# A two-layer graph-attention kernel: step placing and input sums moved from VectorE and ScalarE to GpSimd, the first normalisation halved, keys and values begun before the degrees are known

## The chip, the cores and the metric

One NeuronCore of a Trainium2 chip runs the whole program; the other cores are idle. The metric is the device time of one execution in microseconds (us), and below, times without a unit are microseconds from the start of the profiled execution's span. Engines: TensorE (PE; its weight loads are shown apart as PEld), VectorE (DVE), ScalarE (ACT), GpSimd (POOL) and SyncE (SP, which here only issues transfers). SBUF is the on-chip memory, a PSUM bank holds 128 x 512 float32 of TensorE's results.

## What is computed

3125 nodes with 128 features, 103125 directed edges sorted by target, two layers. The parts that matter here:

```python
h = relu(layernorm(x))                      # the layers' input
for l in range(2):
    xn  = layernorm(x, ln1_g[l], ln1_b[l])
    deg = segment_sum(ones, src); deg = (deg - deg.mean()) / (std(deg) + 1e-6)
    xp  = xn + xn @ Wpos[l] + bpos[l] + deg[:, None] * Wdeg[l][0] + bdeg[l]
    q, k, v = xp @ Wq[l] + bq[l], xp @ Wk[l] + bk[l], xp @ Wv[l] + bv[l]
    att   = clip(nan_to_num((q[dst] * k[src]).sum_per_head / 4), -50, 50)
    alpha = softmax over the edges of one dst
    x = x + segment_sum(v[src] * alpha, dst) @ Wo[l] + bo[l]
    x = x + gelu(layernorm(x, ln2_g[l], ln2_b[l]) @ W1[l] + b1[l]) @ W2[l] + b2[l]
return x_in + x
```

## The kernel before, in words

The nodes are 25 blocks of 128. The edges are tiles of 128, four tiles to a group, 202 groups a layer; for each tile GpSimd issues one indirect DMA (L765) that fetches 128 rows of keys and values (256 floats) from a table in DRAM (`kv_table`) into a ring of eight groups (`kvr`). That makes 1612 gathers for both layers. Group n may be fetched only when the message of group n-8 is done (`s_msg`, L1552). For each group, ScalarE makes one-hot matrices from `relT` (`edge_spread`, L1172 and L1176), TensorE spreads the queries (`edge_q`, L1005), VectorE multiplies and reduces (L1534, L1538, L1552), TensorE sums (L1018), and VectorE adds to `agg` (L1561). Dense work of finished blocks lies between. `relT` has two buffers; each load (`rel_rows`, L610) serves two of the first groups, so groups 0 to 3 use the first two loads and groups 4 and 5 the third.

Before the first gather there is a preparation of some 110 us, whose order is written out by hand:

- VectorE makes a histogram of the edge sources in 16 steps, each two instructions of one-hot digits in bf16 (L1217, 3328 and 2600 elements), which TensorE sums (L792, 26 matmuls a step, `s_hist_oh` and `s_hist_mm`, two buffers). Other work stands between the steps by step number k: the ranking of the blocks (`rank_blocks`), the statistics of the input, the placing of steps (`place_steps`, L1266 to L1294), the scaling of the query weights (`scale_queries`), the folding of the position weights (`fold_positions`, L1314), the first layer's variance (`first_layer_var`, L1239 to L1242).
- ScalarE passes over the input five times, 25 instructions each: sums (L1053), squares about the mean (L1056), normalise and rectify with sums (L1061), squares of that (L1070), the first layer's normalisation (L1076). Then it takes the transposed blocks out of PSUM (L1083), the transposed tile numbers (`rel`, `srcidx`, L1088) and the bias of keys and values (L1091).
- GpSimd waits for `tileno`, the last product that it needs of `place_steps` (L1290), fetches 7 + 7 tiles of targets and sources (L726), splits the biases in three bf16 parts (L730 to L735), and turns the fetched integers to floats and subtracts the block's base (L738, L739, L743, L745). TensorE transposes these (`turn_rows`, L835). A memset of `agg` (L749) follows.
- When the histogram is done, TensorE and ScalarE make the degrees and their spread. Then VectorE writes keys and values for 13 pairs of blocks: for each block degree times weight plus bias (L1368), for each pair the sum with TensorE's product in PSUM (L1381, product L853). SyncE stores each pair to the table (L621). GpSimd's first gather waits for all 13 stores.
- Then come the queries (TensorE L862 with the bias in L780, VectorE L1602 into two buffers `q_nat`), and SyncE moves each block to its rank's place (L627, 25 transfers). The first `edge_q` waits for these.

SyncE issues in program order, and it waits in that order too: behind the row for ranks come 25 transfers of the normalised input to its ranked place (`x`, L591), then biases, `rel_table`, `relT` twice, the 13 stores, the 25 query moves, and then the third `relT`.

## Time and profile before

| | |
|---|---|
| time, median of three (lowest to highest) | 2205.68 us (2205.52 to 2209.19) |
| time of the profiled execution | 2207.93 us |
| span of the profiled execution | 2206.2 us |
| busy in the span: DVE, POOL, PE, ACT | 1716.4, 1578.3, 1417.7, 933.9 us |
| mean granted TensorE clock | 0.807 of full speed |

Times of instructions are those of the profiled execution. A group line gives out<-in by the program's names, the count, busy time and mean, and the idle time of the engine just before these instructions with what ended it. Two instructions on one engine overlap a little, so starts are a better measure of pace than durations.

### The profile page before, as it was taken

How to read it: one execution, taken by the hardware profiler on the slowest of the kernel's cores; microseconds unless marked ns; L12 is line 12 of the kernel's file. 1: busy time of each engine (PE TensorE's matmuls, PEld its weight loads, DVE VectorE, ACT ScalarE, POOL GpSimd, SP SyncE). 2: the span in 40 equal slices, each digit the busy share in tenths (PEclk: the TensorE clock that was granted, in tenths of full speed). 3: DMA queues.
4: the chain of work that ended last, by engine and by line, in shares of the span. 5: the costliest groups of instructions: out<-in, count | busy, mean ns of one | idle time of the engine just before them, and what ended most of it. 6: DMA issues, size and time to landing. Idle time of an engine off the chain costs nothing.

```text
span 2206.2 us, 32470 instructions
## 1 busy us (share of the span) xinstructions
PE 1417.7 (64%) x8220; PEld 1243.9 (56%) x8220; DVE 1716.4 (78%) x5109; ACT 933.9 (42%) x2172; POOL 1578.3 (72%) x1669
## 2 busy tenths in 40 slices
PE   5766566665766666666666656666665766566666
PEld 4555565555655555565555556555555655555564
DVE  7849888887788878887866777777777778777776
ACT  7424353543435353534543334334353435344343
POOL 6277777777777777777726777777777777777773
PEclk9769888888878878877877777778798779778778
DMA  3355444444444444454424444444444444444442
GB/s 101 99 162 164 141 134 148 129 144 134 134 145 128 148 134 143 128 148 134 136 62 125 134 134 134 129 134 138 134 128 134 137 134 128 134 134 138 125 138 57
DMA packets 123505, 289.30 MB, mean 131 GB/s; under 512 B 31524, under 2 KB 57056, under 8 KB 123328
## 3 DMA queue, kind: packets, MB, share of 16 engines
q0 software_dynamic: 77824, 212.31, 33.3%
q1 hardware_dynamic: 45504, 74.92, 10.4%
q8 instruction: 76, 1.25, 0.2%
q14 instruction: 101, 0.83, 0.1%
HBM read 275.44 MB, written 8.38 MB: 129 GB/s over the span
## 4 chain that ended last, share of the span: by engine, by line
POOL 57%; issue 21%; DVE 7%; PE 7%; DMA 4%; ACT 3%; DVEq 0%; POOLq 0%; SPq 0%; ACTq 0%
POOL kvr L765 57%; DMA kvr<-kv_table,srcidx 3%; PE bank L1005 2%; PE bank L1018 2%; DVE agg L1561 2%; DVE kvr L1217 1%; DVE prod L1534 1%; DVE msg L1552 1%; ACT apart L1172 1%; ACT x_nat L1061 1%; ACT onehotT L1176 0%; ACT agg L1076 0%; PE bank L930 0%; DVE kvr L1368 0%; PE bank L949 0%
## 5 line engine op out<-in xcount | busy, mean ns | idle before, releaser
L765 POOL DMA_INDIRECT kvr<-kv_table,srcidx x1612 | 1531.6, 950 | 558.8 <-issue 481.7
L1005 PE MATMUL bank<-q,onehotT 128*128 x3328 | 611.1, 341 | 726.1 <-DVE prod L1534 478.8
L1005 PEld LDWEIGHTS bank<-q,onehotT 128*128 128x128 f32 x3328 | 520.3, 238 | 829.1 <-issue 828.7
L1018 PE MATMUL bank<-msg,onehot 128*128 128x136 f32 x3328 | 609.9, 343 | 3.4 <-DVE msg L1552 3.3
L1181 ACT ACTIVATE bank<-attc 128x32 f32<-128x32 f32 x404 | 81.2, 201 | 1194.0 <-DVE attc L1547 1193.4
L1018 PEld LDWEIGHTS bank<-msg,onehot 128*128 128x128 f32 x3328 | 571.0, 251 | 5.9 <-DVE msg L1552 5.7
L1534 DVE TENSOR_TENSOR prod<-kvr,bank 128x512 f32<-128x512 f32 x404 | 276.9, 685 | 306.6 <-DMA kvr<-kv_table,srcidx 272.6
L1561 DVE TENSOR_TENSOR agg<-agg,bank 128x136 f32 x1628 | 471.6, 290 | 44.7 <-PE bank L1018 38.2
L1172 ACT ACTIVATE apart<-relT,minus_p 128x512 bf16<-128x512 bf16 x416 | 293.8, 706 | 0.5
L1527 DVE TENSOR_TENSOR onehot<-bank,rel 128x512 f32<-128x512 f32 x416 | 283.1, 683 | 0.4
L1552 DVE TENSOR_TENSOR msg<-kvr,bank 128x512 f32<-128x512 f32 x404 | 274.8, 680 | 2.8 <-ACT bank L1181 2.6
L1538 DVE TENSOR_REDUCE att<-prod 128x32 f32<-128x512 f32 x404 | 274.0, 678 | 0.1
L1176 ACT ACTIVATE onehotT<-apart 128x512 f32<-128x512 bf16 x416 | 261.9, 629 | 13.1
L1184 ACT ACTIVATE msg<-attc 128x32 f32<-128x32 f32 x404 | 86.0, 213 | 0.0
L1543 DVE TENSOR_SCALAR attc<-att 128x32 f32<-128x32 f32 x404 | 78.2, 194 | 0.0
L1547 DVE COPY_PREDICATED attc<-attnan,zeros 128x32 f32<-128x32 uint8 x404 | 77.2, 191 | 0.0
L1542 DVE TENSOR_TENSOR attnan<-att 128x32 uint8<-128x32 f32 x404 | 74.6, 185 | 0.1
L1427 DVE TENSOR_TENSOR x<-x,bank 128x384 f32<-128x384 f32 (+1 forms) x36 | 18.9, 525 | 67.6 <-PE bank L780 67.5
L1181 ACT ACT_TABLE_LOAD x52 | 66.7, 1283 | 0.9
L961 PE MATMUL bank<-w,hT 128*128 128x128 f32 x400 | 57.1, 287 | 3.4 <-issue 2.8
L949 PE MATMUL bank<-xnT,w 128*128 128x384 f32 (+1 forms) x144 | 57.6, 531 | 1.6 <-ACT xnT L1112 1.3
L1217 DVE TENSOR_TENSOR kvr<-kvr,q 128x3328 bf16<-128x3328 bf16 (+1 forms) x32 | 53.1, 1715 | 1.7 <-ACT q L1047 1.3
(205 smaller groups left out, 854.6 us busy)
## 6 DMA issues: line engine op xcount, KB each, us to landing
relT<-rel_table SPq DMA_DIRECT2D x104, 512.0 KB, 4.2
kvr<-kv_table,srcidx POOLq DMA_INDIRECT x1612
qkv<-kv_table SPq DMA_DIRECT2D x25, 128.0 KB, 3.4
kv_table<-qkv SPq DMA_DIRECT2D x25, 128.0 KB, 3.0
kv_table<-kvr SPq DMA_DIRECT2D x12, 256.0 KB, 2.1
w<-weights SPq DMA_DIRECT2D x2, 840.0 KB, 7.6
loops<-x_in SPq DMA_DIRECT2D x5, 320.0 KB, 5.6
x<-x_nat SPq DMA_DIRECT2D x25, 64.0 KB
```

The lines of the kernel that those rows point to most:

```text
L765: pool.indirect_dma_start(kvr[:, n % RING, j, :], None, kv_table[l], bass.IndirectOffsetOnAxis(ap=srcidx[:, step:step + 1], axis=0)).then_ ...
L1005: mm = pe.matmul(bank[2][:, j * D:(j + 1) * D], onehotT[:, m % OHT, j, :], q[:, bass.ds(ranks[j + h], 1), :].rearrange("p a c -> p (a c)") ...
L1018: mm = pe.matmul(sum_ps(n, k), onehot[:, m % OH, j, :], msg[:, n % 2, j, :], start=(m, j) == of[0], stop=(m, j) == of[-1])
L1172: act.activation(apart[:], relT[:, m // BODY % 2, r, :], ACT.Abs, bias=minus_p[:]).then_inc(s_apart, 1)
L1176: act.activation(onehotT[:, m % OHT, :, :].rearrange("p j e -> p (j e)"), apart[:], ACT.Relu, bias=1.0, scale=-1.0).then_inc(s_ohT, 1)
L1181: act.activation(ex, attc[:, n % 2, :], ACT.Exp).then_inc(s_ex, 1)
L1184: act.activation(msg[:, n % 2, :, D:AGG], attc[:, n % 2, :].rearrange("p (j h) -> p j h", h=H), ACT.Exp).then_inc(s_den, 1)
L1527: dve.tensor_tensor(onehot[:, m % OH, :, :], iota_ps.unsqueeze(1).broadcast_to([P, G, P]), rel[:, row:row + G].unsqueeze(2).broadcast_to([ ...
L1534: dve.tensor_tensor(prod[:], kvr[:, n % RING, :, 0:D], bank[2][:].rearrange("p (j c) -> p j c", c=D), ALU.mult).then_inc(s_prod, 1)
L1538: dve.tensor_reduce(att[:, n % 2, :], prod[:].rearrange("p j (h d) -> p (j h) d", d=HD), AX, ALU.add).then_inc(s_att, 1)
L1552: dve.tensor_tensor(by_head(msg[:, n % 2, :, 0:D]), by_head(kvr[:, n % RING, :, D:KV]), ex.rearrange("p (j h) -> p j h", h=H).unsqueeze(3) ...
L1561: dve.tensor_tensor(target, target, sum_ps(n, j), ALU.add).then_inc(s_agg, 1)
```

## The change

- `input_sums` (new, GpSimd): the sum over the 128 features of each of 25 blocks as seven tensor additions of 1600, 800, 400, 200, 100, 50 and 25 elements a partition. The ScalarE pass of sums is gone; the pass of squares is about the row's first element instead of its mean, so that it needs no mean, and VectorE corrects for it (`input_var`, four instructions for three).
- `scale_queries` (ten small instructions) and the greater part of `place_steps` (eleven) go to GpSimd. VectorE keeps `begin_blocks` at k = 2 and `number_steps` at k = 4, which waits for GpSimd (`s_within`). `tileno` comes out of `number_steps`. GpSimd fetches the targets, splits the biases, then fetches the sources.
- The first layer's statistics are made in two halves, blocks 0 to 11 (k = 4) and 12 to 24 (k = 8), the reciprocals in the middle of the steps 2, 5 and 9.
- TensorE transposes blocks 0 to 11 at k = 6 and 7, the rest at k = 11 and 12, the tile numbers at k = 13 and 14, all four in bank 5 one after the other. Keys and values of pairs 0 to 3 are made before or beside the degrees, and VectorE keeps them with their bias (`keep_early`); the degree is added for each block when it is known (`add_degrees`, one instruction a block for all 25). Pairs 4 to 12 get the bias from a matmul. The extra pass of L1381 is gone.
- SyncE: the 25 `x` transfers stand behind the query moves, and so ahead of the third `relT`. The second layer's folding comes behind the queries on TensorE and VectorE.

The diff cut to its core:

```diff
+            def input_sums():
+                for k in range(X_LOADS):
+                    pool.wait_ge(s_x[k], 16)
+                half = D // 2
+                pool.tensor_tensor(x_nat[:, :, 0:half], x_raw[:, :, 0:half], x_raw[:, :, half:D], ALU.add).then_inc(s_sums_in, 1)
+                for k in range(1, SUM_STEPS):
+                    half //= 2
+                    pool.wait_ge(s_sums_in, k)
+                    target = x_sums[:, 0, :].unsqueeze(2) if half == 1 else x_nat[:, :, 0:half]
+                    pool.tensor_tensor(target, x_nat[:, :, 0:half], x_nat[:, :, half:2 * half], ALU.add).then_inc(s_sums_in, 1)
...
+            input_sums()
+            scale_queries()
+            place_steps()
+            pool.wait_ge(s_tileno, 1)
+            fetch_rows(step_dst, dst_tiles)
+            split_bias()
+            fetch_rows(step_src, src_tiles)
...
-                act.activation(x_nat[:, b, :], x_raw[:, b, :], ACT.Identity, accum_out=x_sums[:, 0, b:b + 1]).then_inc(s_sums_in, 1)
-            act.wait_ge(s_mean_in, 1)
-            for b in range(BLOCKS):
-                act.activation(x_nat[:, b, :], x_raw[:, b, :], ACT.Square, bias=shift[:, b:b + 1], accum_out=x_sums[:, 1, b:b + 1]).then_inc(s_sums_in, 1)
+                act.activation(xn_nat[:, b, :], x_raw[:, b, :], ACT.Square, bias=x_raw[:, b, 0:1], scale=-1.0, accum_out=x_sums[:, 1, b:b + 1]).then_inc(s_squares_in, 1)
...
+            rectify(*HALVES[0])
+            square(*HALVES[0])
...
+            rectify(HALVES[1][0], middle)
+            first_layer_root(0)
+            rectify(middle, BLOCKS)
+            first_layer_norm(0)
+            square(*HALVES[1])
+            for c in range(3):
+                untranspose_nat(c)
+            first_layer_root(1)
...
             for k in range(HSTEPS):
-                hist_step(k)
+                hist_low(k)
+                if k == 2:
+                    scale_and_shift(0, 0, BLOCKS)
+                elif k == 5:
+                    scale_and_shift(1, *HALVES[0])
+                elif k == 9:
+                    scale_and_shift(2, *HALVES[1])
+                hist_high(k)
...
+                    begin_blocks()
+                elif k == 4:
+                    number_steps()
+                    first_layer_var(0)
...
+            def add_degrees(i):
...
+                    of = to[:, j, :] if i < KV_EARLY else bank[k][:, j * KV:(j + 1) * KV]
+                    ins = dve.scalar_tensor_tensor(out=to[:, j, :], in0=u_deg[:, 0, D:3 * D], scalar=deg[:, 0, b0 + j:b0 + j + 1], in1=of, op0=ALU.mult, op1=ALU.add)
...
-            sp.wait_ge(s_relu, BLOCKS)
-            for b0, nb in NAT:
-                for j, r in enumerate(read_block_ranks(ENG.SP, b0, nb)):
-                    sp.dma_start(x[:, bass.ds(r, 1), :], x_nat[:, b0 + j:b0 + j + 1, :]).then_inc(s_x_ranked, 16)
```

Where instructions stand. On GpSimd, between its constants and the first gather, before:

```order
L716 COPY hT<-ident 64x64 x2
L721 COPY hT<-w 128x128 x2
L726 DMA q<-dst_tiles,tileno 128x128 x7
L726 DMA q<-src_tiles,tileno 128x128 x7
L730 CAST bias_bf<-bias_col 128x10
```

and now, in the same place:

```order
L749 TENSOR_TENSOR x_nat<-loops 128x25x64
L754 TENSOR_TENSOR x_nat<-x_nat 128x25x32
L754 TENSOR_TENSOR x_nat<-x_nat 128x25x16
...
L784 TENSOR_TENSOR onehot<-onehot 128x175
L785 TENSOR_TENSOR onehot<-onehot,ahead 128x175
L786 TENSOR_TENSOR onehot<-onehot,seam_of 128x25
L787 TENSOR_TENSOR onehot<-onehot,seam_tile 128x25
L788 TENSOR_TENSOR onehot<-onehot,number 128x175
L792 DMA q<-dst_tiles,tileno 128x128 x7
L797 CAST bias_bf<-bias_col 128x10
```

28 instructions now stand ahead of the first fetch, and the bias split stands between the fetches. On VectorE, behind the last histogram step (`hT` is `counts`, `deg` the degrees), before:

```order
L1350 COPY hT<-bank 64x50
L1351 COPY hT<-bank 64x50
L1353 SCALAR_TENSOR_TENSOR deg<-bank,valid 128x25
L1355 TENSOR_SCALAR degstd<-degstd 128x1
L1356 RECIPROCAL degstd<-degstd 128x1
L1358 TENSOR_SCALAR deg<-deg,degstd 128x25
L1368 SCALAR_TENSOR_TENSOR kvr<-u_deg,deg,kv_bias 128x256 x4
L1381 TENSOR_TENSOR kvr<-kvr,bank 128x512
L1368 SCALAR_TENSOR_TENSOR kvr<-u_deg,deg,kv_bias 128x256 x2
L1381 TENSOR_TENSOR kvr<-kvr,bank 128x512
```

and now:

```order
L1474 TENSOR_TENSOR onehot<-bank,kv_bias 128x512 x2
L1493 COPY hT<-bank 64x50
L1494 COPY hT<-bank 64x50
L1496 SCALAR_TENSOR_TENSOR deg<-bank,valid 128x25
L1474 TENSOR_TENSOR onehot<-bank,kv_bias 128x512
L1499 TENSOR_SCALAR degstd<-degstd 128x1
L1500 RECIPROCAL degstd<-degstd 128x1
L1502 TENSOR_SCALAR deg<-deg,degstd 128x25
L1474 TENSOR_TENSOR onehot<-bank,kv_bias 128x512
L1486 SCALAR_TENSOR_TENSOR onehot<-u_deg,deg,onehot 128x256 x2
L1486 SCALAR_TENSOR_TENSOR onehot<-u_deg,deg,bank 128x256 x2
```

Four early pairs are kept ahead of and between the degree's instructions, and behind them one instruction a block is left.

## Rows read from the trace of the kernel before

**Rows 1.** The page: chain of work that ended last, and its costliest group.

```profile
POOL 57%; issue 21%; DVE 7%; PE 7%; DMA 4%; ACT 3%; DVEq 0%; POOLq 0%; SPq 0%; ACTq 0%
...
L765 POOL DMA_INDIRECT kvr<-kv_table,srcidx x1612 | 1531.6, 950 | 558.8 <-issue 481.7
```

**Rows 2.** Waits of POOL, whole span: us in total, times, longest.

```profile
POOL kvr L765 <- DMA kv_table<-kvr: 23.0, 1, 23.0
...
POOL kvr L765 <- DVE msg L1552: 9.1, 30, 0.3
```

**Rows 3.** Chain that ended last, 0 to 135: start, us, what.

```profile
18.85 0.10 DVE permrow L1266
...
25.51 0.18 DVE mv L1234
...
106.79 2.10 DMA kv_table<-kvr
...
109.70 1.00 POOL kvr L765
```

**Rows 4.** Timeline of DVE: start, us, engine line op, count, [idle before <-releaser].

```profile
42.24 0.28 DVE L1341 CAST rankT<-bank 7x128 int32<-7x128 f32 x1 [6.37 <-PE bank L826]
...
61.77 1.61 DVE L1241 COPY mv<-x_sums 128x25 f32<-128x25 f32 x1
63.39 4.03 DVE L1217 TENSOR_TENSOR kvr<-kvr,q 128x3328 bf16<-128x3328 bf16 x2
...
67.78 12.98 DVE L1217 TENSOR_TENSOR kvr<-kvr,q 128x3328 bf16<-128x3328 bf16 x8
82.63 0.20 DVE L1350 COPY hT<-bank 64x50 f32<-64x50 f32 x1 [1.86 <-PE bank L792]
...
86.98 0.18 DVE L1353 SCALAR_TENSOR_TENSOR deg<-bank,valid 128x25 f32<-128x25 f32 x1 [3.92 <-PE bank L896]
...
88.91 1.67 DVE L1368 SCALAR_TENSOR_TENSOR kvr<-u_deg,deg,kv_bias 128x256 f32<-128x256 f32 x4
90.50 0.68 DVE L1381 TENSOR_TENSOR kvr<-kvr,bank 128x512 f32<-128x512 f32 x1
```

**Rows 5.** Timeline of POOL, 20 to 67, the same columns.

```profile
23.88 1.13 POOL L726 DMA_INDIRECT q<-dst_tiles,tileno  x1 [8.78 <-DVE tileno L1290]
...
43.17 9.85 POOL L726 DMA_INDIRECT q<-src_tiles,tileno  x1 [0.30 <-issue]
53.02 1.46 POOL L730 CAST bias_bf<-bias_col 128x10 bf16<-128x10 f32 x1
...
56.26 0.21 POOL L733 TENSOR_TENSOR bias_col<-bias_col,bias_bf 128x10 f32<-128x10 f32 x1
...
61.66 1.67 POOL L743 TENSOR_TENSOR onehotT<-onehotT,block 128x896 f32<-128x896 f32 x1
63.40 2.65 POOL L745 CAST prod<-onehotT 128x896 bf16<-128x896 f32 x1
```

**Rows 6.** Timeline of PE, the matmuls.

```profile
85.26 0.26 PE L892 MATMUL bank<-bias,ones 3*128 3x256 bf16 x1 [1.35 <-ACT srcidx L1088]
...
87.87 4.56 PE L853 MATMUL bank<-w,loops 128*128 128x256 f32 x20
```

**Rows 7.** Stretches of 5 us: PE, PEld, DVE, ACT, POOL busy, granted clock, DMA share, GB/s.

```profile
95.00:100.00 5.00, 4.13 (x17) 2.48 (x16) 5.00 (x12) 0.04 (x1) 0.00 (x0) 1.00 0.60 203
...
105.00:110.00 5.00, 5.00 (x17) 3.29 (x17) 4.97 (x12) 0.00 (x0) 0.30 (x1) 0.50 0.53 177
```

**Rows 8.** Timeline of SP, transfers issued.

```profile
110.56 18.72 SPq L627 DMA_DIRECT2D q<-qkv  x25
129.32 0.59 SPq L610 DMA_DIRECT2D relT<-rel_table  x1
```

**Rows 9.** Timeline of ACT and of DVE: groups 4 and 3 of the edges.

```profile
152.95 0.70 ACT L1172 ACTIVATE apart<-relT,minus_p 128x512 bf16<-128x512 bf16 x1
...
162.59 0.68 DVE L1552 TENSOR_TENSOR msg<-kvr,bank 128x512 f32<-128x512 f32 x1
```

More of the change, by code:

```diff
@@ L375, in build @@
         spare = kvr[:].rearrange("p r g c -> p (r g c)")
-        kv_nat = spare[:, G * KV:G * KV + BLOCKS * KV].rearrange("p (b c) -> p b c", c=KV)
+        kv_rest = spare[:, LO + (HI + LO) * HT:]
         spare = spare.bitcast(BF16)
@@ L749, in _ @@
             pool.memset(agg[:], 0.0).then_inc(s_zero, 1)
-            for k in (2, 3):
-                pool.wait_ge(*read(0, k, "rows"))
+            pool.wait_ge(*read(0, 3, "rows"))
             for n in range(L * GROUPS):
@@ L849, in keys_values @@
                 b0, nb = KV_PAIRS[i]
+                if i == 0:
+                    pe.wait_ge(*read(0, 0, "fold"))
+                pe.wait_ge(*read(0, (b0 + nb - 1) // 4, "T"))
                 claim(0, i, "kv")
@@ L1057, in _ @@
             root_var(s_var_in, 1, mv[:, :, 1], std[:], s_std)
-            act.wait_ge(s_shift, 1)
-            for b in range(BLOCKS):
-                act.activation(x_nat[:, b, :], x_raw[:, b, :], ACT.Relu, bias=shift[:, b:b + 1], scale=rstd[:, b:b + 1], accum_out=x_sums[:, 0, b:b + 1]).then_inc(s_relu, 1)
-            act.wait_ge(*full(0, 0, "posT"))
-            act.copy(wposT, bank[TURN[0, 0, "posT"][0]][:, 0:L * D].rearrange("p (l c) -> p l c", l=L)).then_inc(read(0, 0, "posT")[0], 1)
-            for l in range(L):
-                act.wait_ge(*full(0, l, "u"))
-                act.copy(u_deg[:, l, :], bank[TURN[0, l, "u"][0]][:, 0:3 * D]).then_inc(read(0, l, "u")[0], 1)
@@ L1078, in _, with rectify, square @@
-            act.wait_ge(*full(0, 0, "biasT"))
-            act.copy(bias_parts[:], bank[TURN[0, 0, "biasT"][0]][0:PARTS * L * RC, 0:D]).then_inc(read(0, 0, "biasT")[0], 1)
-            for c in range(NATS):
+            def rectify(b0, b1):
+                for b in range(b0, b1):
+                    act.activation(x_nat[:, b, :], x_raw[:, b, :], ACT.Relu, bias=shift[:, b:b + 1], scale=rstd[:, b:b + 1], accum_out=x_sums[:, 0, b:b + 1]).then_inc(s_relu, 1)
+            def square(b0, b1):
+                act.wait_ge(s_relu, b1)
+                act.wait_ge(s_squares_in, BLOCKS)
+                for b in range(b0, b1):
+                    act.activation(xn_nat[:, b, :], x_nat[:, b, :], ACT.Square, accum_out=x_sums[:, 1, b:b + 1]).then_inc(s_squares, 1)
@@ new lines, in first_layer_root, with first_layer_norm @@
+            def first_layer_root(h):
+                b0, b1 = HALVES[h]
+                root_var(s_var0, h + 1, mv[:, b0:b1, 1], std[:, b0:b1], s_std)
+            def first_layer_norm(h):
+                b0, b1 = HALVES[h]
+                act.wait_ge(s_shift, h + 2)
+                act.wait_ge(s_squares, b1)
+                for b in range(b0, b1):
+                    act.activation(xn_nat[:, b, :], x_nat[:, b, :], ACT.Identity, bias=shift[:, b:b + 1], scale=rstd[:, b:b + 1]).then_inc(s_xn_nat, 1)
@@ L1187, in _ @@
             edge_spread(1)
+            for l in range(1, L):
+                keep_degree(l)
             for l in range(L):
@@ new lines, in add_degrees @@
+            def add_degrees(i):
+                b0, nb = KV_PAIRS[i]
+                k = TURN[0, i, "kv"][0]
+                to = kv_of(b0, nb)
+                if i < KV_EARLY:
+                    dve.wait_ge(*read(0, i, "kv"))
+                else:
+                    dve.wait_ge(*full(0, i, "kv"))
+                for j in range(nb):
+                    of = to[:, j, :] if i < KV_EARLY else bank[k][:, j * KV:(j + 1) * KV]
+                    ins = dve.scalar_tensor_tensor(out=to[:, j, :], in0=u_deg[:, 0, D:3 * D], scalar=deg[:, 0, b0 + j:b0 + j + 1], in1=of, op0=ALU.mult, op1=ALU.add)
+                ins.then_inc(s_kv_early if i < KV_EARLY else s_read[k], 1)
@@ L1348, in _ @@
+            dve.wait_ge(*read(0, 0, "wide"))
+            keep_early(0)
+            keep_early(1)
             dve.wait_ge(s_hist_mm, HSTEPS)
@@ L1587, in _ @@
             dve.tensor_copy(iota_ps, iota_free[:]).then_inc(s_iota_ps, 1)
-            dve.wait_ge(s_iota_ps, 1)
-            for k in range(2):
-                dve.wait_ge(*read(0, k, "rows"))
-            edge_onehot(0)
-            edge_onehot(1)
             def queries_nat(c):
@@ L1607, in _ @@
                 queries_nat(c)
+                if c == 1:
+                    dve.wait_ge(s_degT_ps, 1)
+                    dve.tensor_copy(degT, degT_ps).then_inc(s_degT, 1)
+                elif c == 3:
+                    dve.wait_ge(s_degR_ps, 1)
+                    dve.tensor_copy(deg[:, 1, :], degR_ps).then_inc(s_degR, 1)
+                    dve.wait_ge(s_first_table, 16 * len(KV_PAIRS))
+                    dve.wait_ge(s_iota_ps, 1)
+                    for k in range(2):
+                        dve.wait_ge(*read(0, k, "rows"))
+                    edge_onehot(0)
+                    edge_onehot(1)
+            for l in range(1, L):
+                fold_positions(l)
             dve.wait_ge(s_rel_table, 16)
```

361 lines of the change are left out of this document (204 added, 157 removed).

## The prediction

> **What bounds the kernel now.** I read the chain of waits first. GpSimd holds 57% of it with one line, L765, the gathers, and the 21% called issue is mostly the gap between two of them [rows 1]: 1612 gathers of 0.950 busy and 0.30 between (481.7 of idle time over them), 1.253 each, 2020 in all. Then the waits of GpSimd: in the loop almost none is for data. Messages release it 30 times for 9.1 in all, never over 0.3, which is the ordinary gap [rows 2]. So the ring of eight groups is always free in time, and the gathers run at their own pace from the first, at 109.70, to the end of their layer. The change does not touch that pace. It can only move the first gather, whose releaser is the last store of keys and values [rows 2, 3], and the start of the edge loop behind it. Whatever the first gather gains, the end gains, as long as the first groups' messages keep up.
>
> Next, what the first gather waits for. VectorE writes the histogram until 67.78 + 12.98 = 80.76; its sums arrive at 82.63; the degrees at 86.98 after a wait of 3.92; keys and values from 88.91 [rows 4] to about 106.4; store 106.79 for 2.10, gather 109.70 [rows 3]. The wait of 3.92 was ScalarE's: TensorE stood until ScalarE had copied the source numbers [rows 6].
>
> Last, how VectorE and GpSimd get on. A copy of 25 elements at 61.77 takes 1.61 while GpSimd's L743 runs for 1.67 from 61.66; a histogram pair at 63.39 takes 4.03, where four pairs take 12.98, 3.25 each; and a GpSimd cast of 10 elements takes 1.46 at 53.02, one addition of that size 0.21 [rows 4, 5]. Each lasts until the other engine's instruction ends: the two exclude each other. The Trainium skill says the same (SBUF — State Buffer, section on the two separate sides: the pair of ports is an exclusive lock, held for the whole instruction). Its rule speaks against this change: work handed to GpSimd in the histogram does not leave VectorE's time.
>
> **The change part by part.** VectorE's own work up to the end of the histogram. Placing steps and scaling ran from 18.85 to 25.51 [rows 3], 32 instructions; 13 stay, among them most of the wide ones, so 3.3 of 6.7 stay: -3.4. The wait of 6.37 for the transposed ranks goes [rows 4], because they are asked for five steps later: -6.4. The exclusion seen above goes at that place: -1.4 and -0.8. Five small instructions more at 0.2 and one fold less: +0.5. 80.8 becomes 69.3.
>
> What GpSimd puts back. Rate: L743, 896 elements with two inputs, 1.67; a tiny one 0.21 [rows 5]; so 1.65 ns an element and 0.2 fixed. Input sums: 3175 elements in seven instructions, 5.2 + 1.4 = 6.6, begun when the input has landed, in the middle of two histogram pairs and the ranking, which stand meanwhile. Ten scalings of 0.2: 2.0. Placing, eleven instructions (three of 175 elements): some four get in between the histogram's instructions of k = 3 and 4 (0.9), the rest is what VectorE waits for at k = 4 (2.0). Bias split, seven: 1.4. The three casts and L743: the casts with one input at half the rate, 0.8 each, 4.1 together. Sum 17.0, and the histogram ends at 86.3. Bounds: nothing at all if GpSimd only waited and never held, 69.3 plus a wait of 2, 71; and 2.9 more if the memset of `agg` (no row shows one against the histogram) holds VectorE too, 89.2. I take 86.3, since every cast above shows the exclusion.
>
> By the skill (GPSIMD Engine Reference, on elementwise operations: an addition of 2048 float32 takes 4497 ns) the seven sums would be an estimated 7.0 + 1.4 = 8.4, not 6.6.
>
> GpSimd's own queue is the second path. The first fetch was at 23.88 [rows 5], after three histogram steps. Now `tileno` comes after five: +6.5; sums, scalings, placing and wait +11.5; less placing on VectorE -1: about 41. The 14 fetches took from 23.88 to 53.02, 9.85 of it in one; the other 13 took 1.48 each [rows 5]. Now 14 at 1.48, 20.7; the split, seven instructions behind a histogram instruction each (1.46 for the cast at 53.02), 8.5; landing 2; then casts and L743, four waits and 3.3 of work, to the point that TensorE waits for, 7.5: about 80. TensorE then needs four round trips through bank 5 (some 1.2 each) with two histogram steps of 1.4 and small matter between, 8.3: histogram summed at 88.3. VectorE's path gives 86.3 + 1.9 = 88.2 (the wait at 82.63 was 1.86). The two paths are equal, by chance.
>
> From there to the gather. TensorE makes pair 2 (one of five pairs in 4.56 [rows 6]: 0.9) and the degree product: degrees at +1.65, where it was +4.35. To the first addition 1.93 as before [rows 4], and one kept pair that nothing covers, 0.6; the kept pairs 0, 1 and 2 lie in waits (1.86, and that for the spread). Then 25 additions at 1.67 / 4 = 0.40 each [rows 4], 10.0 for what took 17.4. Source in PSUM for 17 of them: I take the same price, the one row of the other kind (0.68 for 512 elements from PSUM) being no dearer per element. Store and start 3.3. In all 17.6: gather at 105.8, 3.9 earlier. TensorE's products with their bias row at about 1.3 a pair end just before VectorE's last.
>
> Does the loop follow? Group 11 may be fetched after message 3. It ended at 162.59 + 0.68 = 163.3 [rows 9], and that gather stood at 109.70 + 44 x 1.253 = 164.8: only 1.5 to spare. Message 3 follows group 4's one-hots (152.95), and these need the third `relT`, issued at 129.32 behind 25 query moves of 18.72 [rows 8]. Now 25 `x` transfers of the same kind, 18.7, stand before it. The old margin of 23.6 less some 4 for landing shrinks to about 1. And TensorE's clock stood at 0.50, its lower level of 1.2 GHz, in 105 to 110, and at 1.00, 2.4 GHz, in 95 to 100 [rows 7]; the queries run in that low stretch, and they bring the loop forward by less than the gather. I take a stall of 0.8, between 0 and 1.5.
>
> Sum: -3.9 + 0.8 = -3.1. Against the profiled execution, 2207.93 (span 2206.2): 2204.8. That execution is 2.25 above the median, so 2205.7 - 3.1 = 2202.6. A measurement of this kernel tells about 0.2% (4.4) from no change, so this is "the same, slightly below".
>
> **The rivals.** *B, the engines get on better.* The histogram's pairs may often slip past GpSimd, as fetches take 1.48 and not 1.6 more; input sums may fall on waits. With half of the 17.0 put back and the fetches earlier too, everything comes 8 earlier but the loop's start, which is tied to the same chain: -3.1 - 8 + 2 for new waits of TensorE or ScalarE = -9, 2196.6. For it: nothing else in the chain is fixed. Against: all shown pairs exclude.
>
> *C, slower: a starved fetch.* The fetch at 43.17 took 9.85 while VectorE ran six histogram instructions without a gap, and ended after the first gap [rows 4, 5]. Now steps 11 to 15 are such a run, 16 long, and VectorE has few gaps earlier. If one source fetch starves there, it ends only when the histogram does; the numbers are ready at about 89 instead of 80, TensorE has two histogram steps still to sum behind them, and the gather comes at 114.8: 5.1 later, 2210.8. It decides from 83.8 on: later than that and the kernel loses. [...]
>
> *D, the loop does not follow.* The gather is earlier, but `relT` or the queries are late, or TensorE's clock is low already in keys and values (half speed: 2 a pair, nine pairs, 4 to 6 more). The gain is given back: 2204 to 2208, say 2206.
>
> **How the numbers follow.** Forecast 2202.6, chance 0.45, its own range 2199 to 2206; B 0.27; C 0.13; D 0.15. Faster by over 0.2%: B and a fifth of the forecast, 0.36. Slower by over 0.2%: C and a third of D, 0.17 with a remainder. Same 0.47. Range: down to B, and up to C, 2196.5 to 2210.5.
>
> **What would show it.** In the new profile: the first gather at about 106 with the store of the last pair just ahead; VectorE's ranking stretched by some 6 while the seven sums run; a wait of about 2 at `number_steps`; the first fetch at about 41; TensorE waiting for the transposable numbers at about 80; VectorE's additions 0.40 apart; GpSimd waiting once, for 1 or less, near the 44th gather. I am wrong if histogram instructions are not stretched by GpSimd (B), if a fetch lasts over 5 (C), or if gathers wait for a message for more than 2 in the first 60 (D).

## The result, and the profile after

The changed kernel takes 2216.24 us (median of five, 2215.37 to 2216.93), the kernel before 2205.68 (2203.19 to 2209.19): ratio 1.0042, 95% interval 1.0031 to 1.0053. It is slower by 0.42%, 10.6, where 3.1 less was forecast. The profiled run is one of 2216.93, with a span of 2215.2 where it was 2206.2.

First come the page's chain that ended last and its costliest group, then the waits of GpSimd over the whole span (total, times, longest). They answer [rows 1, 2].

```profile
POOL 51%; issue 20%; PE 12%; DVE 8%; DMA 4%; ACT 3%; SPq 1%; DVEq 1%; ACTq 0%; POOLq 0%
...
L839 POOL DMA_INDIRECT kvr<-kv_table,srcidx x1612 | 1528.3, 948 | 565.5 <-issue 482.0
```

```profile
POOL kvr L839 <- DMA kv_table<-xn: 27.3, 1, 27.3
POOL kvr L839 <- DVE msg L1678: 10.9, 28, 2.7
```

A gather still costs 0.948 and its gap 0.30 (482.0 over 1612). So the loop's pace is what it was (the gathers together take 3.3 less, 1528.3 for 1531.6), and the loss lies ahead of the first gather, except one wait of 2.7. The timeline of GpSimd (start, us, engine line op, count, [idle before <-releaser]) shows where; it answers [rows 5, 3].

```profile
39.14 1.22 POOL L792 DMA_INDIRECT q<-dst_tiles,tileno  x1 [1.07 <-DVE tileno L1413]
...
61.04 1.12 POOL L792 DMA_INDIRECT q<-src_tiles,tileno  x1 [0.30 <-issue]
62.47 16.01 POOL L792 DMA_INDIRECT q<-src_tiles,tileno  x1 [0.30 <-issue]
78.79 0.94 POOL L792 DMA_INDIRECT q<-src_tiles,tileno  x1 [0.30 <-issue]
...
86.01 1.68 POOL L818 TENSOR_TENSOR onehotT<-onehotT,block 128x896 f32<-128x896 f32 x1
...
118.84 0.99 POOL L839 DMA_INDIRECT kvr<-kv_table,srcidx  x1 [27.28 <-DMA kv_table<-xn]
```

One fetch lasts 16.01. The first gather comes at 118.84, 9.1 later than in [rows 3]. The timeline of VectorE over the same stretch answers [rows 4]:

```profile
7.63 9.91 DVE L1342 TENSOR_TENSOR kvr<-kvr,q 128x3328 bf16<-128x3328 bf16 x4 [1.30 <-ACT q L1145]
...
28.07 6.54 DVE L1342 TENSOR_TENSOR kvr<-kvr,q 128x3328 bf16<-128x3328 bf16 x4
38.10 0.33 DVE L1411 TENSOR_REDUCE tile_f<-onehot 128x7 f32<-128x175 f32 x1 [3.48 <-POOL onehot L788]
...
61.26 0.27 DVE L1467 CAST rankT<-bank 7x128 int32<-7x128 f32 x1
61.47 16.19 DVE L1342 TENSOR_TENSOR kvr<-kvr,q 128x3328 bf16<-128x3328 bf16 x10
97.87 1.29 DVE L1474 TENSOR_TENSOR onehot<-bank,kv_bias 128x512 f32<-128x512 f32 x2 [20.22 <-ACT kv_bias L1218]
99.08 0.19 DVE L1493 COPY hT<-bank 64x50 f32<-64x50 f32 x1
...
115.47 0.48 DVE L1486 SCALAR_TENSOR_TENSOR xn<-u_deg,deg,bank 128x256 f32<-128x256 f32 x1
```

The histogram ends at 61.47 + 16.19 = 77.66, well ahead of the 86.3 forecast, and VectorE then stands idle for 20.22. The fetch ends at 78.48, 0.8 behind it; before, the fetch of 9.85 ended at 53.02, also 0.8 behind VectorE's end (42.45 + 9.74 = 52.19). TensorE shows who was waited for (timeline of the matmuls; [rows 6] are those of before):

```profile
87.75 1.11 PE L911 MATMUL bank<-ident,onehotT 128*128 128x128 f32 x4 [15.13 <-POOL onehotT L818]
...
101.72 0.28 PE L854 MATMUL bank<-bias,ones 3*128 3x256 bf16 x1
101.92 0.70 PE L932 MATMUL bank<-w,loops 128*128 128x256 f32 x2
102.56 0.28 PE L854 MATMUL bank<-bias,ones 3*128 3x256 bf16 x1
102.77 0.70 PE L932 MATMUL bank<-w,loops 128*128 128x256 f32 x2
```

It stood for 15.13 until GpSimd's subtraction (L818) had made the numbers it transposes, with the last two histogram steps, two kept pairs and the spread of the bias queued behind in its own order. Later a block of keys and values costs 0.84 (101.72 to 102.56), 1.69 a pair.

### The profile page after: what moved, and what is told of

Same layout as the page of the kernel before. It is cut to its first block, busy times and chain, and to the rows that moved or that the text cites. A ratio compares the mean times of both kernels' runs of the same rounds, so it can differ in the third digit from the quotient of the medians.

```text
span 2215.2 us, 32464 instructions
## 1 busy us (share of the span) xinstructions
PE 1429.7 (65%) x8237; PEld 1251.8 (57%) x8237; DVE 1713.9 (77%) x5086; ACT 928.0 (42%) x2123; POOL 1604.1 (72%) x1695
## 4 chain that ended last, share of the span: by engine, by line
POOL 51%; issue 20%; PE 12%; DVE 8%; DMA 4%; ACT 3%; SPq 1%; DVEq 1%; ACTq 0%; POOLq 0%
POOL kvr L839 49%; PE bank L1103 4%; PE bank L1116 3%; DMA kvr<-kv_table,srcidx 3%; DVE agg L1687 3%; POOL q L792 2%; DVE prod L1660 1%; PE bank L854 1%; ACT apart L1299 1%; ACT onehotT L1303 1%; PE bank L948 1%; PE bank L932 1%; DVE msg L1678 1%; SPq L651 1%; PE bank L1038 1%
## 5 line engine op out<-in xcount | busy, mean ns | idle before, releaser
L839 POOL DMA_INDIRECT kvr<-kv_table,srcidx x1612 | 1528.3, 948 | 565.5 <-issue 482.0
L1116 PE MATMUL bank<-msg,onehot 128*128 128x136 f32 x3328 | 617.6, 346 | 3.9 <-DVE msg L1678 3.9
L1116 PEld LDWEIGHTS bank<-msg,onehot 128*128 128x128 f32 x3328 | 579.2, 254 | 5.6 <-DVE msg L1678 5.4
```

The lines of the kernel that those rows point to most:

```text
L839: pool.indirect_dma_start(kvr[:, n % RING, j, :], None, kv_table[l], bass.IndirectOffsetOnAxis(ap=srcidx[:, step:step + 1], axis=0)).then_ ...
L1116: mm = pe.matmul(sum_ps(n, k), onehot[:, m % OH, j, :], msg[:, n % 2, j, :], start=(m, j) == of[0], stop=(m, j) == of[-1])
```

## The experiments

The undisturbed kernel before is timed beside each, and a ratio is the experiment's time over that of the kernel before. Runs e1 to e4 and e9 to e12 fell on two chips where TensorE is granted about 0.68 on average instead of 0.81 and the kernel before takes 2815; there the gathers wait for messages over 200 times, 610 to 640 in all, so the time does not follow the first gather. From those chips I use the preparation's traces (the starved fetch lasts 16.01 to 16.02 there and on the others), and repeat some of the runs on other chips for their time. Their ratios there were 0.9988 (e1), 1.0045 (e3), 1.0019 (e4), 1.0024 (e9) and 1.0056 (e11); e3, e9 and e11 were not timed where the gathers bound the loop, so for these three the first gather is all that is shown.

**e4 and e8, gaps in the histogram.** One copy of a column behind each of the last ten histogram instructions:

```diff
+                elif k >= 11:
+                    link(dve.tensor_copy(key[:, 0:1], key[:, 1:2]))
                 hist_high(k)
+                if k >= 11:
+                    link(dve.tensor_copy(key[:, 0:1], key[:, 1:2]))
```

> The changed kernel, with one tiny VectorE copy (128 x 1, waited for) behind each of the ten histogram instructions of steps 11 to 15, so that VectorE is never without a gap there. Theory (a fetch is starved by histogram instructions that follow one another without a gap): the fetch that took 16.0 from 62.5 now ends after one or two histogram instructions, under 3.5; the numbers are ready at 76 to 80 instead of 87.7, the histogram ends at 80 to 84 instead of 77.7, TensorE's wait in front of the numbers falls from 15.1 to under 6, and the first gather comes at 108 to 112 instead of 118.8: 2206 to 2210. Rival (the fetch is held by something else, such as the queue's own descriptors or the transfers of the other queues): the fetch still takes over 8, and the time is that of the changed kernel plus up to 3 for the copies, 2216 to 2219.

Timeline of GpSimd in e4:

```profile
61.94 1.69 POOL L792 DMA_INDIRECT q<-src_tiles,tileno  x1 [0.30 <-issue]
63.93 1.30 POOL L792 DMA_INDIRECT q<-src_tiles,tileno  x1 [0.30 <-issue]
...
72.36 2.59 POOL L814 CAST onehotT<-q 128x896 f32<-128x896 int32 x1
74.91 2.94 POOL L818 TENSOR_TENSOR onehotT<-onehotT,block 128x896 f32<-128x896 f32 x1
```

The starving is gone; the numbers are ready at 77.9 instead of 87.7, the histogram ends at 81.7, 4.0 later (ten gaps, and casts that now exclude VectorE), and the first gather is at 109.10. The same kernel once more, where the gathers bound the loop:

> The kernel of e4_breaks once more, unchanged: there TensorE was granted 0.683 of its clock over the whole run, and waits in the edge loop hid what the preparation gained, though the first gather had come at 109.10 instead of 118.84. Theory (the time follows the first gather where the gathers bound the loop): the first gather at 109 again, and where the kernel before takes some 2206, this takes 2206 to 2208, ratio 1.000 within 0.001. Rival (the loop's start or another wait takes the gain): over 2210.

```profile
108.45 0.99 POOL L839 DMA_INDIRECT kvr<-kv_table,srcidx  x1 [25.05 <-DMA kv_table<-xn]
```

The first gather of e8 is at 108.45, and the time is 2206.53 against 2207.01, ratio 0.9999 (0.9989 to 1.0009). Ten copies of no use take back the whole loss, although they lengthen the histogram. The starved fetch is its cause.

**e11, placing back on VectorE.** All of `place_steps` and `number_steps` at k = 2 again, everything else as changed:

```diff
-            place_steps()                      # GpSimd
             pool.wait_ge(s_tileno, 1)
...
                     begin_blocks()
+                    place_steps()
+                    number_steps()
                 elif k == 4:
-                    number_steps()
```

> The changed kernel with one part undone: `place_steps` (eleven small instructions) and `number_steps` are back on VectorE behind step 2; input sums and scalings stay on GpSimd. Theory (putting the placing on GpSimd delayed the first fetch by 7 to 8, and so pushed the source fetches into the run without a gap): the first fetch at 31 to 32 instead of 39.1, the last source fetch is through before step 11, none starves, the numbers are ready at 66 to 72, TensorE has transposed them before the histogram ends at 78 to 81, the first gather at 100 to 104 instead of 118.8, and the time 2199 to 2204, with waits for messages of up to 3. Rival (another fetch starves earlier, or GpSimd's casts now fall on the histogram and give back as much): numbers after 76, histogram after 83, gather after 106, 2205 or more.

A miss, and the most useful one: the fetches begin at 31.00, eight earlier, and fewer are left, yet one starves (timeline of GpSimd):

```profile
59.37 1.11 POOL L768 DMA_INDIRECT q<-src_tiles,tileno  x1 [0.30 <-issue]
60.79 16.02 POOL L768 DMA_INDIRECT q<-src_tiles,tileno  x1 [0.30 <-issue]
```

It is again the first fetch issued after the copy of the transposed ranks (59.59 here). First gather 113.72. So the starving is not a matter of how late the fetches come, and the copy itself had to be tried.

**e7 and e9, the copy earlier and last.** In e7 the cast to `rankT` stands one step earlier (behind step 9); in e9 it stands behind the last histogram step, and its transfer on SyncE behind it.

```diff
-                elif k == 10:
+                elif k == HSTEPS - 1:
                     dve.wait_ge(*full(0, 0, "rankT"))
```

> The changed kernel, with VectorE's cast of the transposed ranks one histogram step earlier (behind step 9 instead of 10), so that VectorE has no gap from about 58 to the end of the histogram. In the kernel before and in the changed one the starved fetch was the first that was issued after this cast. Theory (any fetch can lose in a run without a gap; which of them does is a matter of where it meets the histogram instructions): the fetches at 56.8 and 59.3, which went through between two histogram instructions, now may starve, and the one that does starve ends 0.8 behind the end of the histogram; the first gather moves by less than 5. Rival (the cast, or the transfer of the ranks behind it, sets it off): the fetch issued next after the cast starves, at about 58 to 60, for 18 to 20, and four more stand behind it, the first gather some 3 to 4 later.

> The changed kernel, with VectorE's cast of the transposed ranks behind the last histogram step instead of behind step 10 (its PSUM bank is then 4), and with it SyncE's transfer of the ranks behind the bias transfers. No gap is added to the histogram; one is taken away, so that VectorE has none from 56.6 to the end. So far the starved fetch was in all three kernels that had one (before, changed, e7_cast_early) the first that was issued behind this cast. Theory A (a run without a gap is enough): one of the fetches issued from 56.8 on starves until 0.8 behind the histogram, 16 to 20, and the first gather comes at 118 to 121, 2216 to 2220. Theory B (the cast, or the ranks' transfer behind it, sets it off): no fetch takes over 3, the numbers are ready at 76 to 80 as in e8_breaks_again, the first gather comes at 107 to 110, 2205 to 2208.

Timelines: GpSimd in e7, VectorE in e9, GpSimd in e9.

```profile
59.16 19.19 POOL L792 DMA_INDIRECT q<-src_tiles,tileno  x1 [0.31 <-issue]
```

```profile
56.22 24.54 DVE L1342 TENSOR_TENSOR kvr<-kvr,q 128x2600 bf16<-128x2600 bf16 x13
```

```profile
56.42 2.17 POOL L792 DMA_INDIRECT q<-src_tiles,tileno  x1
58.90 1.45 POOL L792 DMA_INDIRECT q<-src_tiles,tileno  x1 [0.31 <-issue]
60.65 1.12 POOL L792 DMA_INDIRECT q<-src_tiles,tileno  x1 [0.30 <-issue]
62.08 1.50 POOL L792 DMA_INDIRECT q<-src_tiles,tileno  x1 [0.30 <-issue]
63.88 1.12 POOL L792 DMA_INDIRECT q<-src_tiles,tileno  x1 [0.30 <-issue]
```

With the copy earlier the first fetch after it starves for 19.19, over twelve histogram instructions, and the gather is at 120.62 (2220.69, one run). With the copy last, thirteen histogram instructions follow one another without a gap and all seven source fetches get through, the first in 2.17 and the others in 1.50 at most: gather 108.03. A run without a gap is not enough to starve a fetch, as my rival C had it; the copy is needed too. VectorE's thirteen took 24.54 where 21.0 would be normal (16.19 / 10 each): 3.5 for the casts and the subtraction that now fall on them.

**e13, e14, e18, e17: what of the copy.** e13 moves only the ranks' transfer on SyncE away. e14 leaves that away and copies float to float, the cast to integers coming last. e18 has the cast between the two instructions of step 10. e17 is e14 with the copy over all 128 partitions of the bank instead of 7:

```diff
-                    dve.tensor_copy(rank_f[:], bank[TURN[0, 0, "rankT"][0]][0:SC, 0:P])
+                    dve.tensor_copy(rank_f[:], bank[TURN[0, 0, "rankT"][0]][:, 0:P])
```

> The changed kernel, with SyncE's transfer of the ranks (128 B to 512 B rows, 0.94 to issue) moved from behind the cast to just ahead of `rel_table`; VectorE's cast of the ranks stays behind histogram step 10. In e9_cast_last, where cast and transfer were both late, no fetch starved in a run of 13 histogram instructions without a gap. If the cast sets it off: the fetch at about 62 takes 16 again, gather at 118. If the transfer sets it off: no fetch over 3, numbers ready at 76 to 80, gather at 107 to 110.

> The changed kernel, with the cast of the ranks split: behind step 10 VectorE copies them from PSUM as float32 (same shape, same place), and the cast to int32 (now from SBUF) and SyncE's transfer come behind the histogram. If any small instruction from PSUM at that place sets the starving off: the fetch at about 62 takes 16, gather at 118. If it is the cast to int32 (or the transfer behind it): no fetch over 3, numbers ready at 76 to 80, gather at 107 to 110.

> The changed kernel, with the cast of the ranks between the two histogram instructions of step 10 instead of behind the second; 11 histogram instructions without a gap then follow it. If what follows the cast starves wherever it stands (as in e7_cast_early, two instructions earlier): the fetch at about 59 to 61 takes 16 to 19, the first gather at 118 to 121. If its place between two steps decides (the next instruction being the longer one): no fetch over 3, numbers ready at 76 to 80, gather at 107 to 110.

> The kernel of e14_float_copy, with the copy behind step 10 over all 128 partitions of the bank instead of 7 (the other 121 are not used). If the few partitions set the starving off: no fetch over 3, the first gather at 107 to 110. If any small copy at that place does: the fetch at about 62 takes 16 again, gather at 118.

The copy on VectorE and the next fetch on GpSimd, of e14 and then of e17:

```profile
61.12 0.27 DVE L1469 COPY rank_f<-bank 7x128 f32<-7x128 f32 x1
...
62.32 16.01 POOL L794 DMA_INDIRECT q<-src_tiles,tileno  x1 [0.31 <-issue]
```

```profile
60.82 0.28 DVE L1469 COPY rank_f<-bank 128x128 f32<-128x128 f32 x1
61.02 19.89 DVE L1344 TENSOR_TENSOR kvr<-kvr,q 128x3328 bf16<-128x3328 bf16 x10
...
62.02 1.70 POOL L794 DMA_INDIRECT q<-src_tiles,tileno  x1 [0.30 <-issue]
```

e13 starves for 16.01 (gather 116.97), so it is not the transfer; e14 for 16.01 (118.49), so not the type; e18 for 17.43 over eleven instructions (118.45), so not the place between steps. e17 has the same copy at the same distance from the fetch (1.20 in both) and as long (0.28 to 0.27), only over 128 partitions: 1.70, numbers at 77.0, gather 107.62. These four are single runs, of 2213.85, 2216.64, 2215.36 and 2211.80; the kernel before took 2210.72 beside the first two and 2207.15 beside the others. In e17 the gather is 2.1 earlier than before and the time 4.7 longer: gathers wait 16.2 for messages, 5.2 at the longest, where before it was 9.1 and 0.3. This is the price that rival D named: once the gather is early, the loop's start is what comes late.

**e2, e12 and e16, `x` early.** The 25 `x` transfers stand ahead of `rel_table` again, behind the biases:

```diff
+            sp.wait_ge(s_relu, BLOCKS)
+            for b0, nb in NAT:
+                ... (x's 25 transfers, unchanged)
             sp.wait_ge(s_rel_bf, 1)
             sp.dma_start(rel_table...
```

> The changed kernel, with SyncE's 25 `x` transfers directly behind the three bias transfers (62.6 to 64.9 in the changed kernel, after which SyncE stands until 88.7) instead of behind the query moves. Theory (the third `relT` comes late behind them; ScalarE waits 2.3 for it at 165.9, and GpSimd 2.7 for a message at 176.3): the first gather stays at 118.8, both waits go, the time falls by 2.4: 2213.8. Rival (the edge loop starts late because the queries are late, 138.9, and the `relT` only shares that): the wait for the message stays above 1, and the time falls by under 1.2: 2215 to 2216.

> The kernel of e2_x_early a third time, unchanged; both earlier tests fell on a chip where GpSimd waited 26 for a message at 183. Theory (the third `relT` came late behind the 25 `x` transfers): the first gather at 118 to 119, no wait for a message above 0.5 in the first 60 gathers, the time 1.5 to 3 below the changed kernel's, ratio 1.0030 to 1.0042. Rival (late queries hold the loop): a wait of 1 or more stays, and the ratio is that of the changed kernel, 1.0042 or more.

e2 and its repetition e12 gave 1.0053 (1.0030 to 1.0076) and 1.0057 (1.0037 to 1.0077) on the chips that wait for messages anyway: inconclusive. e16, where the gathers bound: third `relT` issued at 137.06 instead of 159.42, and no gather waits over 0.3 (8.5 in all, 28 times, against 10.9). First gather 117.57, ratio 1.0035 (1.0022 to 1.0048). The wait of 2.7 goes with the 25 transfers: in e7, e8, e13, e14 and e18, which leave them in place, the longest wait is 1.3 to 2.3. The first `edge_q` comes earlier too, 140.35 for 144.94, while the first gather gains 1.3. A gain in time is not shown, as 1.0035 and 1.0042 lie within each other's interval.

**e3, the bias once a pair.** One matmul of 3x512 ahead of a pair in place of two of 3x256 behind its blocks:

```diff
+                    of_pair = bias3[:, R_QKV + 1:R_QKV + 3, :].rearrange("k c e -> k (c e)").unsqueeze(1).broadcast_to([PARTS, nb, KV])
+                    pe.matmul(use(0, i, "kv")[:, 0:nb * KV], ones3[:], of_pair, start=True, stop=False)
...
-                        mm = bias_row(o, 0, R_QKV + 1, 2)
```

> The changed kernel, with one bias product of 512 columns for a pair of blocks (pairs 4 to 12) in place of two of 256. In the changed kernel each block took 0.84 on TensorE with its bias product (101.92 to 115.36, granted clock 1.00), and in the kernel before 0.46 without one, so the product costs 0.38 a block. Theory (TensorE bounds keys and values, since VectorE waits 0.6 to 0.8 at each pair from the eighth on): the fixed part of that cost is paid once a pair, a pair takes 1.3 to 1.5 instead of 1.69, the first gather comes 1.8 to 3.4 earlier, 2213 to 2214.5. Rival (the cost goes with the columns): 1.69 a pair as before, no change, 2216.

Matmuls of e3:

```profile
99.58 0.39 PE L932 MATMUL bank<-bias,ones 3*128 3x512 bf16 x1
99.89 1.13 PE L935 MATMUL bank<-w,loops 128*128 128x256 f32 x4
100.95 0.38 PE L932 MATMUL bank<-bias,ones 3*128 3x512 bf16 x1
101.27 1.13 PE L935 MATMUL bank<-w,loops 128*128 128x256 f32 x4
```

1.38 a pair (99.89 to 101.27) instead of 1.69; VectorE's waits for TensorE in its additions fall from 3.0 in all to 0.9. Gather 114.90, 3.9 earlier. Of this 1.6 stands ahead of the counts (97.48 for 99.08; the numbers were ready 0.7 earlier), and only the other 2.3 is the bias product's.

**e1 and e5, numbers not in the way.** The four transpositions of the numbers go behind the last pair, each in a bank of its own, and ScalarE's copies behind the degrees. In e5 the stores of keys and values also stand ahead of `rel_table` and `relT` on SyncE.

```diff
                 elif k == 13:
-                    turn_rows(0)
-                    turn_rows(1)
                     keys_values(1)
                 elif k == 14:
-                    turn_rows(2)
-                    turn_rows(3)
                     spread_bias()
...
                 keys_values(i)
+            for k in ROWS_ORDER:
+                turn_rows(k)
```

> The changed kernel, with the four transpositions of the tile numbers (`turn_rows`) moved on TensorE from behind histogram steps 13 and 14 to behind the last pair of keys and values, each in a bank of its own, and ScalarE's copies of them behind the degrees. The starved fetch is left as it is. Theory (TensorE's order: the fetch is late, but it costs only because TensorE stands in front of the numbers with the last histogram steps and the pairs behind them; in the changed kernel this wait was 15.1, from 72.6 to 87.75): VectorE ends the histogram at 77.7, counts at about 79.5, pairs 4 to 12 from about 81 at 1.69 a pair (101.11 to 115.36 for 17 blocks in the changed kernel), the last addition at about 97, the first gather at about 99 to 101 instead of 118.84: 2196 to 2200, with up to 3 more if the edge loop cannot follow. Rival (the numbers gate the gather themselves, through the source numbers): they are ready at 87.7, need some 9 to be transposed and copied, and nothing would be before 99 either, so a gather past 105 would speak for a third cause. Rival (the cost is not the wait at all but GpSimd's share in VectorE's time): no change, 2214 to 2217.

> The kernel of e1_rows_late, with SyncE's transfers of `rel_table` and the first two `relT` moved behind the 13 stores of keys and values. In e1_rows_late the first gather came at 109.39 although VectorE's last addition stood at 97.11, and the stores took 6.5 each to land (2.2 in the changed kernel), right behind the two `relT` transfers that were issued at 91.29. Theory (the stores queue behind the `relT` transfers): a store lands in 2 to 3 again, the first gather comes at 99.5 to 102, 17 to 19 before the changed kernel's; on a chip that runs the kernel before in some 2206 this is 2196 to 2201. Rival (the source numbers gate the gather: they were copied at 97.69 and 98.2 in e1_rows_late, or the stores are slow for their own number): the gather stays above 105, 2203 to 2208.

```profile
79.03 0.20 DVE L1494 COPY hT<-bank 64x50 f32<-64x50 f32 x1 [0.39 <-PE bank L869]
```

In both the fetch starves for its 16.01 and nobody waits for it: VectorE has the counts at 79.03 in e1 (the line above), where the changed kernel has them at 99.08. But e1's gather is only at 109.39, a miss: SyncE issued the first store at 92.22, behind `relT` at 91.29 for 0.88, and the stores took 6.5 to land (median; 2.2 in e5 and in the changed kernel). e5 stores from 86.24 and gathers at 100.56, 9.1 earlier than before. It wins next to nothing: 2204.62, ratio 0.9989 (0.9980 to 0.9998). Waits of e5, ScalarE from 100 to 200, then GpSimd, whole span:

```profile
ACT apart L1300 <- DMA relT<-rel_table: 10.6, 2, 6.5
```

```profile
POOL kvr L842 <- DVE msg L1679: 16.8, 31, 7.4
```

`relT`, now last, is late, so the first messages are late, and a gather stands 7.4 near 163: the gain is given back in the loop.

**e6, e10 and e15, all together.** e6 is e5 with e3's bias and the early `x`. e15 (and e10) also has `rel_table` between the stores and the two first `relT` behind two of the query chunks:

```diff
+                if at == 6:
+                    sp.wait_ge(s_rel_bf, 1)
+                    sp.dma_start(rel_table...).then_inc(s_rel_table, 16)
...
+                if c == 2:
+                    sp.wait_ge(s_rel_table, 16)
+                    rel_rows(0)
+                    rel_rows(1)
                 sp.wait_ge(*read(0, c, "q"))
```

> The kernel of e5_stores_first with two edits more: one bias product a pair (in its first test a pair took 1.38 instead of 1.69, and the first gather came 3 earlier) and SyncE's `x` transfers behind the bias transfers. Theory (the starved fetch costs nothing once nobody stands behind it; TensorE's pace bounds keys and values; the third `relT` held the loop): the first gather at 97 to 99, no wait for a message above 1, and the time 8 to 12 below the kernel before: 2194 to 2198 where that takes 2206. Rival (VectorE's additions, stretched by GpSimd's casts, 1.96 and 2.18 instead of 0.87 in e1_rows_late, bound instead): the gather at 99.5 to 101, 2197 to 2200.

> The kernel of e10_queries_soon once more, unchanged. There the first gather came at 100.56 and the moves of the queries began at 99.45 instead of 101.14, on a chip where the edge loop waited for messages anyway. Theory (where the gathers bound the loop, SyncE's queue sets the loop's start): the first `edge_q` at 122 to 127 instead of 129.9, waits for messages under 2 together in the first 60 gathers, 2197 to 2200 where the kernel before takes some 2206, ratio 0.996 to 0.9975. Rival (no gain over e6_all): ratio 0.9974 to 0.9985.

e6: gather 99.56, longest wait for a message 3.0, 2201.24 against 2207.01, ratio 0.9974 (0.9965 to 0.9984). e15: gather 100.55, first `edge_q` at 127.40 (129.89 in e6), again a wait of 3.0, where under 2 in all was expected; 2202.53 against 2210.72, ratio 0.9962 (0.9949 to 0.9976). Both beat the kernel before by their ratios, and so the changed one; the intervals overlap, so the order of e15 is not shown to be better than that of e6. e10, the same kernel as e15 on a chip that waits for messages, gave 1.0004 (0.9985 to 1.0022), no difference.

## Why the prediction was wrong

**What bounds the kernel: right.** The time follows the first gather and the gathers' waits for messages beyond the 9.1 of before. Changed kernel: +9.1 + 1.8 = 10.9, measured 10.6 between medians and 9.0 between the two profiled executions (in whose spans the gathers themselves took 3.3 less). By ratio times 2206: e5 -9.1 + 7.7 = -1.4, measured -2.4; e6 -10.1 + 4.3 = -5.8, measured -5.7; e8 -1.3 + 0.9 = -0.4, measured -0.2; e16 +7.9 - 0.6 = 7.3, measured 7.7. Of the repeated runs only e15 is off, -5.3 for -8.4, and its interval (-11.3 to -5.3) just reaches it. The single executions of e13, e14 and e18 lie 4 to 5 below such a sum, but one execution tells little: the kernel before spreads over 10.7 beside the first two.

**VectorE's own work: right.** 77.65 less what GpSimd gave back (9.0, below) leaves 68.65; 69.3 was forecast. The histogram also began 0.8 later than before (7.63 for 6.80); with that taken off it is 67.8.

**What GpSimd puts back: half of it.** Forecast 17.0, found 9.0. The input sums were nearly as forecast: four histogram instructions took 9.91 for 6.54, two ranking ones 1.66 and 0.91 for 0.19 each, some 5.5 together for 6.6. GpSimd paid as well, as its seven sums ran from 10.91 to 22.26, 11.3 for 6.6. The wait at `number_steps` was 3.48 for 2.0. The rest cost VectorE nothing: the scalings (1.94 and 1.50 beside them), the placing (6.54 for four, as always) and the bias split gave no longer histogram instruction. Between engines it was not even: at 28.26 and 31.67 two GpSimd instructions of 25 elements took 3.33 and 3.12, beside VectorE's unstretched four. I had read the exclusion of [rows 4, 5] as a price that VectorE pays; in a run of its long instructions it is GpSimd that pays. The casts' 4.1 did not fall on the histogram, as the starved fetch pushed them past its end; where they do, they cost 3.5 (e9) and 3.7 (e17: 19.89 for 16.19).

**GpSimd's queue: the step that failed.** First fetch 39.14 for 41. "Now 14 at 1.48": thirteen were 0.94 to 2.17, and one was 16.01. Without it the numbers would have been ready at 77 (e9 76.9, e17 77.0) for 80 forecast, since the bias split took 5.3 for 8.5 (it is six instructions, not seven); TensorE had them at 87.75. This is rival C with its price: numbers at 89 forecast, gather 114.8. I gave it 0.13, though [rows 4, 5] held every sign of it: a copy of 7x128 at 42.24, six instructions without a gap, the fetch of 9.85 at 43.17, and no other fetch as long. The change put ten instructions behind that same copy where there had been six. I took the 9.85 as one mishap in fourteen. In all sixteen traces here that have the copy over 7 partitions directly ahead of a gap-free run of the histogram, or between two of its instructions, one fetch starved (9.85 before, 16.0 to 19.2 in the fifteen others), and in the four without (e4 and e8, e9, e17) no fetch of the preparation took over 2.2.

**From numbers to counts: 11.3 for 8.3.** TensorE had stood, and the granted clock was at its lower level, 1.2 GHz, when it began. At that level the histogram step at 92.00 took 2.37, where the next one took 1.36 at the full clock, and the kept pair at 90.30, which the forecast had among small matter, 1.91 for 1.09: 1.8 of the 3.0. In e13, where the clock was 0.80 on average in 90 to 95, the same stretch of work took 10.3. Stretches of 5 us in the changed kernel (busy PE, PEld, DVE, ACT, POOL, granted clock, DMA share, GB/s), as [rows 7]:

```profile
85.00:90.00 5.00, 1.48 (x6) 1.11 (x7) 0.00 (x0) 0.59 (x1) 4.93 (x5) 0.50 0.06 15
90.00:95.00 5.00, 5.00 (x37) 4.31 (x35) 0.00 (x0) 0.48 (x1) 1.56 (x1) 0.50 0.42 119
95.00:100.00 5.00, 3.57 (x40) 2.68 (x39) 1.61 (x4) 1.44 (x3) 0.00 (x0) 0.99 0.37 125
```

With e1 and e5, which take the whole trip out of the way, the counts come 20 earlier: the trip through one bank was the chain's, and 7.7 of lateness and 3.0 of slowness are what the sum lacked ahead of the histogram (99.1 for 88.3).

**From counts to the gather: 19.8 for 17.6.** "About 1.3 a pair end just before VectorE's last" failed: 1.69 a pair at the full clock, so TensorE, not VectorE, set the pace at the end, and VectorE waited 3.0 in four waits. The bias matmul was priced as a trifle; it costs 0.38 a block (0.84 for a block that takes 0.46 where it has none). e3 shows the other price, 1.38.

**The stall: right in kind, 2.4 for 0.8.** GpSimd stood once for more than its gap, 2.69 ahead of the gather at 176.32, for message 3 (it ended at 175.37 + 0.68 = 176.05), at the place forecast:

```profile
176.32 0.95 POOL L839 DMA_INDIRECT kvr<-kv_table,srcidx  x1 [2.69 <-DVE msg L1678]
```

The third `relT` was issued at 159.42 behind `x`, and in e16 the wait goes with the `x` transfers. The query moves took 21.79 for the 18.7 assumed.

**The sum.** -3.9 forecast for the gather; +7.7 numbers, +3.0 to the counts, +2.2 to the gather: +9.0, measured +9.1. That the histogram ended 8.7 earlier than thought gave nothing, since the two paths were not equal and only the later one counts. One slip in the chances changes nothing: C and a third of D are 0.18, not 0.17.

**What stays open.** It is open why a copy over 7 partitions lets the next fetch starve and one over 128 does not; that it does not rests on one execution (e17). The Trainium skill (SBUF — State Buffer, section on the two separate sides) has the lock of the port pair held for a whole instruction by whichever engine starts first. That would fit a fetch that waits for one histogram instruction: 1.1 to 2.2 here, where it takes 0.94 with VectorE idle. It does not tell why ten in a row won each time in one kernel and lost by turns in another. Nor was it tried whether 32 or 64 partitions are enough, or whether a copy from SBUF does it.

## What to carry to other kernels

One long instance among fourteen like ones in a trace can be a mechanism: look at what stood ahead of it, and ask whether the change makes the run it fell into longer. When work goes to GpSimd beside long VectorE instructions, price the wait on GpSimd's side first (here a tiny instruction took up to 3.3, a fetch 16), and keep what TensorE must have next out of that queue; here a result that nobody had to wait for yet (e5) made the same starved fetch free. A first gather made 9 earlier was worth 2 (e5) and one made 10 earlier 6 once the `x` transfers behind it had been moved up as well (e6).

## What the runs showed of the hardware

- A GpSimd fetch can lose every change of instruction on VectorE: 16.01 over ten instructions, 17.43 over eleven, 19.19 over twelve. It came only where the last thing ahead of the fetch, other than histogram instructions, was a copy from PSUM over 7 partitions; with 128 partitions the fetch took 1.70 (e17, one execution), without the copy 1.50 at the same place (e9), with 0.15 of other work between the instructions 1.69 (e4).
- A fetch that starved ended 0.8 behind the last of VectorE's run, in both kernels (78.48 for 77.66, 53.02 for 52.19).
- Stores of 256 KB issued behind two `relT` loads of 512 KB landed after 6.5 instead of 2.2 (e1).
- A tensor addition of 896 elements a partition takes GpSimd 1.68 with VectorE idle (changed kernel) and 2.94 beside the histogram (e4).
